# Causal mask of an attention kernel: maxima masked on VectorE by one add-and-max instruction, transposed scores masked by one fp32r matmul per head and step, batch loop unrolled

## What is computed

```
x = x + tanh(g_xattn) * wkv(w, u, layernorm(x), ctx)
s = layernorm(x);  h1 = rmsnorm(s, ln1);  h = rmsnorm(s, ln2)
scores = einsum('bqhd,bkhd->bhqk', h1 @ Wq.T, h1 @ Wk.T) / sqrt(32)     # 16 heads of 32
scores = where(causal, scores, finfo.min)
attn = (softmax(scores) @ v).reshape(b, s, d) @ Wo.T
mod = 0.1 * tanh(attn @ A)                                              # rank 16
gate = silu(h @ W_in.T + mod * (h @ A) @ B);  mlp = (gate * (h @ W_up.T)) @ W_down.T
x = x + tanh(g_ffn) * (s + mlp)
```

## Time and profile before

| | |
|---|---|
| device time, median of 3 runs | 1065.28 us (1063.98 to 1066.85) |
| span of the profiled execution, which is its own time here | 1067.0 us |
| TensorE busy | 946.0 us, 89% |
| VectorE busy | 641.0 us, 60% |
| ScalarE, GpSimd busy | 412.6 us and 343.2 us, 39% and 32% |
| mean granted clock | 0.933 |

### The profile page before, as it was taken

One profiled execution on the slowest core, in us unless ns is written; L12 is line 12 of the kernel. 1 busy time (PEld: TensorE's weight loads), 2 busy tenths in 40 slices (PEclk: granted clock), 3 DMA queues, 4 the chain that ended last, 5 costly groups with the idle time before them and its releaser, 6 DMA issues. The chain is left out here.

```text
span 1067.0 us, 13783 instructions
## 1 busy us (share of the span) xinstructions
PE 946.0 (89%) x4880; PEld 728.0 (68%) x4880; DVE 641.0 (60%) x1032; ACT 412.6 (39%) x725; POOL 343.2 (32%) x202
## 2 busy tenths in 40 slices
PE   3129999889899999898899999988899999999998
PEld 3127656777788766587688866677688875678886
DVE  7987653698456852678636864478835765232223
ACT  2406454222234555333233654333222555433331
POOL 7540011565440001365542001256544000254441
PEclk9559989899899989999899998999999998999999
DMA  9001213322222210522221220421222221122321
GB/s 280 32 1 40 47 35 112 107 63 85 90 89 72 61 41 2 188 79 70 89 81 49 81 66 18 150 97 60 89 78 78 72 52 41 50 89 94 102 80 42
DMA packets 33548, 81.37 MB, mean 76 GB/s; under 512 B 5648, under 2 KB 5648, under 8 KB 32400
## 3 DMA queue, kind: packets, MB, share of 16 engines
q1 hardware_dynamic: 33472, 80.41, 24.5%
HBM read 63.35 MB, written 4.19 MB: 63 GB/s over the span
## 5 line engine op out<-in xcount | busy, mean ns | idle before, releaser
L373 POOL TENSOR_TENSOR gu_lo<-raw_gu,gu_hi 128x1024 fp32r<-128x1024 f32 x64 | 153.2, 2394 | 589.4 <-ACT gu_hi L487 589.4
L913 PE MATMUL ps<-h_hi,gu_hi 128*128 128x512 f32 x512 | 205.6, 402 | 5.0 <-DVE gsil L867 5.0
L914 PE MATMUL ps<-h_lo,gu_hi 128*128 128x512 f32 x512 | 202.4, 395 | 0.0
L915 PE MATMUL ps<-h_hi,gu_lo 128*128 128x512 f32 x512 | 202.3, 395 | 0.0
L805 DVE TENSOR_REDUCE mx<-ps 128x1 f32<-128x512 f32 (+3 forms) x256 | 112.5, 484 | 74.3 <-PE ps L1006 73.6
L591 ACT ACTIVATE act_hi<-prod 128x512 fp32r<-128x512 f32 x64 | 40.4, 632 | 253.3 <-DVE prod L872 253.3
L867 DVE SCALAR_TENSOR_TENSOR gsil<-th,ps 128x512 f32<-128x512 f32 x64 | 43.3, 677 | 141.0 <-ACT th L587 141.0
L545 ACT ACTIVATE e_row<-ps 128x512 f32<-128x512 f32 (+1 forms) x192 | 90.8, 521 | 92.5 <-PE ps L1026 91.7
L377 POOL TENSOR_TENSOR wd_lo<-raw_d,wd_hi 128x512 fp32r<-128x512 f32 x64 | 94.1, 1470 | 90.4 <-ACT wd_hi L493 90.4
L913 PEld LDWEIGHTS ps<-h_hi,gu_hi 128*128 128x128 f32 x512 | 97.1, 190 | 30.2 <-DVE gsil L867 9.0
L915 PEld LDWEIGHTS ps<-h_hi,gu_lo 128*128 128x128 f32 x512 | 96.6, 189 | 22.7
(11 more groups left out here) (156 smaller groups left out, 1630.5 us busy)
## 6 DMA issues: line engine op xcount, KB each, us to landing
raw_gu<-w_gu_dram SPq DMA_DIRECT2D x64, 512.0 KB, 3.3
raw_d<-w_down_dram SPq DMA_DIRECT2D x64, 256.0 KB, 3.0
x_sb<-x_dram SPq DMA_DIRECT2D x16, 256.0 KB, 3.6
vT<-ctxT_dram SPq DMA_DIRECT2D x4, 1024.0 KB, 8.9
q_st<-q_st SPq DMA_DIRECT2D x16, 256.0 KB, 2.9
k_st<-k_st SPq DMA_DIRECT2D x16, 256.0 KB, 2.9
out_dram<-base SPq DMA_DIRECT2D x16, 256.0 KB, 2.1
q_st<-q_lo SPq DMA_DIRECT2D x32, 64.0 KB, 2.0
```

What stands on the lines that cost most here:

```text
L373: pool.tensor_tensor(gu_s[f % 2][1][:], raw_gu[f % 2][:], f32(gu_s[f % 2][0][:]), ALU.subtract).then_inc(gu_lo, 1)
L913: pe.matmul(dst, w_hi, m_hi, start=start, stop=False)
L914: pe.matmul(dst, w_hi, m_lo, start=False, stop=False)
L915: return pe.matmul(dst, w_lo, m_hi, start=False, stop=stop)
```

## The change

The mask matmuls of scores(n) go; VectorE adds the mask itself while it takes the maximum, with `tensor_tensor_reduce`: it reads the scores from PSUM and a bf16 mask row from SBUF, adds them, writes the sum back to PSUM, and puts the maximum into `mx`. The mask of scores_T becomes an fp32r matmul, one for both blocks of a step (256 columns) where there are two, and one for the one block (128 columns) where there is one: 48 a batch instead of 64. Only the first matmul of such a step clears its bank. The values of a head lie 17 columns apart instead of 32, which changes the layout of `v_aug`. All engines' loops over batches are unrolled.

```diff
-VW = 32
+VW = R + 1
+VROW = H * VW + 16
-MASKED = -1e30
+MASKED, LOWEST = -1e30, -3e38
+ST_FIRST = [0, P, 0]
...
-        identb = place("identb", [P, P], BF16)
-        mask_qk = place("mask_qk", [P, P], BF16)
-        mask_kq = place("mask_kq", [P, P], BF16)
+        ident_r = place("ident_r", [P, P], F32R)
+        mask_kq = place("mask_kq", [P, 2, P], F32R)
+        mask_row = place("mask_row", [P, T], BF16)
...
-        v_aug = place("v_aug", [P, TB, H, VW], F32)
+        v_aug = place("v_aug", [P, TB, VROW], F32)
...
 # on each of the five engines
-            with sp.Fori(0, NB - 1) as b:
-                batch(b, False)
-            batch(NB - 1, True)
+            for b in range(NB):
+                batch(b, b == NB - 1)
...
 # GpSimd, constants
-            pool.affine_select(out=mask_qk[:], in_=mask_qk[:], compare_op=ALU.is_ge, fill=MASKED, base=0,
+            pool.affine_select(out=mask_row[:, T - P:T], in_=mask_row[:, T - P:T], compare_op=ALU.is_ge, fill=MASKED, base=0,
...
+            pool.wait_ge(const_rdy, 3)
+            pool.tensor_copy(ident_r[:], ident[:]).then_inc(const_rdy, 1)
+            pool.memset(v_aug[:], 0.0).then_inc(pool_own, 1)
             pool.wait_ge(pool_own, 4)
-            pool.tensor_copy(identb[:], ident[:]).then_inc(const_rdy, 1)
-            pool.memset(v_aug[:], 0.0).then_inc(pool_own, 1)
-            pool.wait_ge(pool_own, 5)
-            pool.memset(v_aug[:, :, :, R:R + 1], 1.0).then_inc(const_rdy, 1)
+            for tb in range(TB):
+                op = pool.memset(v_aug[:, tb, 0:H * VW].rearrange("p (h r) -> p h r", r=VW)[:, :, R:VW], 1.0)
+            op.then_inc(const_rdy, 1)
...
 # ScalarE, values
-                    act.activation(v_aug[:, tb, :, 0:R], ps[:, bank, 0:H * R].rearrange("p (h r) -> p h r", r=R), ACT.Copy)
+                    act.activation(v_aug[:, tb, 0:H * VW].rearrange("p (h r) -> p h r", r=VW)[:, :, 0:R], ps[:, bank, 0:H * R].rearrange("p (h r) -> p h r", r=R), ACT.Copy)
...
 # VectorE, maxima
-                            op = dve.reduce_max(mx[:, qb, j:j + 1], ps[:, s_bank(n) + i, at:at + (qb + 1) * P], AX.X)
+                            w = (qb + 1) * P
+                            op = dve.tensor_tensor_reduce(ps[:, s_bank(n) + i, at:at + w], ps[:, s_bank(n) + i, at:at + w], mask_row[:, T - w:T], 1.0,
+                                                          LOWEST, ALU.add, ALU.max, mx[:, qb, j:j + 1])
...
 # TensorE, scores
-                            pe.matmul(ps[:, s_bank(n) + i, at:at + w], q_st[g % 3][0:96, j, blk(qb)], k_st[g % 3][0:96, j, 0:w], start=True, stop=False)
-                            op = pe.matmul(ps[:, s_bank(n) + i, at + w - P:at + w], identb[:], mask_qk[:], start=False, stop=True)
+                            op = pe.matmul(ps[:, s_bank(n) + i, at:at + w], q_st[g % 3][0:96, j, blk(qb)], k_st[g % 3][0:96, j, 0:w], start=True, stop=True)
...
 # TensorE, scores_T
-                                      q_st[g % 3][0:98, 2 * pr + i, kb * P:T], start=True, stop=False)
-                            op = pe.matmul(ps[:, st_bank(m) + i, at:at + P], identb[:], mask_kq[:], start=False, stop=True)
+                                      q_st[g % 3][0:98, 2 * pr + i, kb * P:T], start=at == ST_FIRST[s], stop=False)
+                        blocks = len(ST_STEPS[s])
+                        op = pe.matmul(ps[:, st_bank(m) + i, 0:blocks * P], ident_r[:], mask_kq[:, 0:blocks, :], start=False, stop=True)
                         op.then_inc(st_ps, 1)
...
 # TensorE, weigh
-                            op = pe.matmul(ps[quad(j), 6, kb * P:T], v_aug[:, kb, 4 * g + j, :], e_row[g % 2][:, j, E_AT[kb]:E_AT[kb] + w],
+                            op = pe.matmul(ps[quad(j), 6, kb * P:T], v_aug[:, kb, (4 * g + j) * VW:(4 * g + j) * VW + 32], e_row[g % 2][:, j, E_AT[kb]:E_AT[kb] + w],
```

More of the change, by code:

```diff
@@ L328, in _ @@
             pool.memset(ident[:], 0.0).then_inc(pool_own, 1)
-            pool.memset(mask_qk[:], 0.0).then_inc(pool_own, 1)
-            pool.memset(mask_kq[:], 0.0).then_inc(pool_own, 1)
+            pool.memset(mask_row[:], 0.0).then_inc(pool_own, 1)
+            pool.memset(f32(mask_kq[:]), 0.0).then_inc(pool_own, 1)
             pool.memset(minus_half[:], -0.5).then_inc(const_rdy, 1)
@@ L333, in _ @@
             pool.affine_select(out=ident[:], in_=ident[:], compare_op=ALU.not_equal, fill=1.0, base=0,
-                               pattern=[[-1, P]], channel_multiplier=1).then_inc(pool_own, 1)
-            pool.affine_select(out=mask_qk[:], in_=mask_qk[:], compare_op=ALU.is_ge, fill=MASKED, base=0,
                                pattern=[[-1, P]], channel_multiplier=1).then_inc(const_rdy, 1)
-            pool.affine_select(out=mask_kq[:], in_=mask_kq[:], compare_op=ALU.is_ge, fill=MASKED, base=0,
-                               pattern=[[1, P]], channel_multiplier=-1).then_inc(const_rdy, 1)
+            pool.affine_select(out=mask_row[:, T - P:T], in_=mask_row[:, T - P:T], compare_op=ALU.is_ge, fill=MASKED, base=0,
+                               pattern=[[-1, P]], channel_multiplier=1).then_inc(const_rdy, 1)
+            pool.affine_select(out=mask_kq[:], in_=f32(mask_kq[:]), compare_op=ALU.is_ge, fill=MASKED, base=0,
+                               pattern=[[0, 2], [1, P]], channel_multiplier=-1).then_inc(const_rdy, 1)
             pool.iota(steps[:], [[1, T]], base=0, channel_multiplier=0,
                       allow_small_or_imprecise_dtypes=True).then_inc(const_rdy, 1)
+            pool.wait_ge(const_rdy, 3)
+            pool.tensor_copy(ident_r[:], ident[:]).then_inc(const_rdy, 1)
+            pool.memset(v_aug[:], 0.0).then_inc(pool_own, 1)
             pool.wait_ge(pool_own, 4)
-            pool.tensor_copy(identb[:], ident[:]).then_inc(const_rdy, 1)
-            pool.memset(v_aug[:], 0.0).then_inc(pool_own, 1)
-            pool.wait_ge(pool_own, 5)
-            pool.memset(v_aug[:, :, :, R:R + 1], 1.0).then_inc(const_rdy, 1)
+            for tb in range(TB):
+                op = pool.memset(v_aug[:, tb, 0:H * VW].rearrange("p (h r) -> p h r", r=VW)[:, :, R:VW], 1.0)
+            op.then_inc(const_rdy, 1)
             pool.memset(tcols[:], 0.0).then_inc(const_rdy, 1)
@@ L426, in batch @@
                             scales_of_x1(b + 1)
-            with pool.Fori(0, NB - 1) as b:
-                batch(b, False)
-            batch(NB - 1, True)
+            for b in range(NB):
+                batch(b, b == NB - 1)
         @block.scalar
@@ L446, in _ @@
                 kexp_step(0, cb, True)
-            act.wait_ge(const_rdy, 9)
+            act.wait_ge(const_rdy, 10)
             act.wait_ge(woa_ps, 1)
@@ L599, in batch @@
                     normed(b + 1)
-            with act.Fori(0, NB - 1) as b:
-                batch(b, False)
-            batch(NB - 1, True)
+            for b in range(NB):
+                batch(b, b == NB - 1)
         @block.vector
@@ L728, in _ @@
             dve.tensor_scalar(half_gate[:], gate_t[:, 1:2], 0.5, None, ALU.mult)
-            dve.wait_ge(const_rdy, 5)
+            dve.wait_ge(const_rdy, 6)
             for cb in range(DB):
@@ L902, in batch @@
                 assert last or own["n"] == DVE_OWN_PER_BATCH, own["n"]
-            with dve.Fori(0, NB - 1) as b:
-                batch(b, False)
-            batch(NB - 1, True)
+            for b in range(NB):
+                batch(b, b == NB - 1)
         @block.tensor
@@ L940, in normed_T @@
                 op.then_inc(hnT_ps, 1)
-            pe.wait_ge(const_rdy, 6)
+            pe.wait_ge(const_rdy, 3)
             for cb in range(DB):
@@ L963, in _ @@
             pe.wait_ge(ones_rdy, 3)
-            pe.wait_ge(const_rdy, 8)
+            pe.wait_ge(const_rdy, 9)
             def batch(b, last):
@@ L1165, in batch @@
                 down(NF - 1)
-            with pe.Fori(0, NB - 1) as b:
-                batch(b, False)
-            batch(NB - 1, True)
+            for b in range(NB):
+                batch(b, b == NB - 1)
 def kernel(x, ctx_2048, g_xattn, g_ffn, L0_xattn_w, L0_xattn_u, L0_ffn_ln1_w, L0_ffn_ln2_w, L0_ffn_Wq, L0_ffn_Wk,
```

## The result

The changed kernel takes 1069.96 us (median of 9, 1069.12 to 1072.3), the kernel before 1065.28 (median of 9). The ratio is 1.0048, 95% interval 1.0031 to 1.0065: slower by half a per cent, where 1046 us was forecast. Runs more than 1.5% above the fastest of their kernel are left out of all ratios here, which concerns three runs of experiment 2 and no others.

What follows compares the result with a forecast made beforehand. TensorE was taken as the limit, VectorE co-limiting in steps 0 to 9. 5.4 us a batch gave 21.5, plus 0.9 loop, less 3.0 clock: 19.4 off 1067.0, less 1.7 to the median, 1046 us; range 1037 to 1054, chance 0.52.

Steps and rivals of the forecast that it cites:

- x = 0.10: VectorE: each add-and-max costs 0.10 us more than a plain reduction; 8.8 less 34 times that saves 5.4 a batch.
- x = 0: VectorE: delivering the reduced value adds nothing per instruction; 8.8 us saved a batch; with the clock held 1029 us, chance 0.13.
- Steps 10 to 15 are bound by TensorE ... together 2.9: Attention, steps 10 to 15: 2.04 us saved on scores and 0.84 on transposed scores, together 2.9 a batch.
- steps 18 to 20 run at the half clock ... doubled 2.5: Attention, steps 18 to 20: TensorE's saving of 1.26 us a batch counts double at the half clock, 2.5.
- Of its idle 2.56 us I keep 0.7, so 1.86 - 28x are saved: Steps 0 to 9: VectorE becomes the limit; 1.86 us a batch saved, less the added cost of 28 add-and-max instructions.
- so such a fall costs 1.5 ... 3 us lost: Scores phase: batch 1's clock fall costs 1.5 us and comes in batches 2 and 3 too, 3 us lost.
- Rival 2: Attention: clock falls more often as TensorE waits for VectorE, six more falls at 1.5 us, 1055 us; chance 0.14.
- Rival 3: Attention: VectorE becomes the bound, each add-and-max costing 0.28 us more through a drained read, 1072 us; chance 0.14.
- Rival 4: Attention: gains and losses cancel, TensorE's saving seen in busy time and nowhere in the span, 1062 to 1068; chance 0.07.
- The signs named beforehand: Prediction wrong if add-and-max adds above 0.24 us, an fp32r mask matmul exceeds 0.12, or clock falls where it now holds.
- The merged mask: Transposed scores: fp32r mask matmuls save 0.21 us a head over 64 heads, at 0.12 us per 256-column mask.
- The loop: Batch seams: unrolling brings gaps of 0.80 and 0.56 us to 0.24, saving 0.9 us in total.

Runs made afterwards that it cites:

- experiment 2: Changed kernel with reduce_max in place of the add-and-max and both masks' fill 0: 1058.4 us, median of six; ratio 0.9826 from three of them.
- before (12): Kernel before, unchanged, profiled a second time: one run of 1065.62 us, span 1063.8.
- experiment 5: Changed kernel plus 30 idle matmuls a batch where TensorE waited: 1049.07 us, ratio 0.9823 to the kernel before.
- experiment 7: Changed kernel with old score masks and reduce_max in steps 0 to 9, 16 and 17, plus 17 idle matmuls a batch: 1041.36 us, ratio 0.9759.
- experiment 9: Kernel before with loops unrolled, masks as they were, plus 17 idle matmuls a batch: 1051.53 us, ratio 0.9843.
- reduce_max, busy (10): Changed kernel with reduce_max, masks' fill 0 and 30 idle matmuls a batch: 1037.95 us, ratio 0.9725 to the kernel before.
- (3): Changed kernel with the transposed scores' masks as before, bf16 matmuls of 128 columns, one per block: 1075.23 us, ratio 1.0100 to the kernel before.
- (1): Kernel before with its five batch loops unrolled and nothing else: 1067.73 us, ratio 1.0037.

## Why the prediction was wrong

The starts of the batches, of scores, of transposed scores and of the first matmul of L1080 (other line numbers in the other kernels) cut each trace into stages. Their lengths, summed over the four batches (us, numbers of experiments in the heads; the columns add to the spans; the first row is the prologue and each batch's matmuls ahead of its first scores):

| stage | before | before (12) | changed | reduce_max (2) | busy (5) | hybrid, busy (7) | before, busy (9) | reduce_max, busy (10) |
|---|---|---|---|---|---|---|---|---|
| up to the first scores | 128.6 | 130.5 | 130.2 | 129.1 | 129.1 | 129.2 | 128.3 | 128.9 |
| steps 0 to 9 | 92.1 | 92.1 | 96.8 | 89.4 | 97.0 | 92.2 | 92.1 | 90.6 |
| steps 10 to 15 | 75.5 | 72.4 | 75.2 | 73.3 | 68.8 | 67.2 | 72.1 | 67.9 |
| steps 16 to 20 | 66.9 | 66.6 | 64.5 | 60.6 | 50.6 | 50.8 | 52.0 | 48.8 |
| steps 21 to 23 | 26.2 | 26.2 | 25.1 | 25.0 | 26.2 | 25.1 | 26.2 | 24.7 |
| tail | 85.8 | 85.8 | 84.0 | 85.3 | 89.1 | 84.0 | 85.8 | 84.1 |
| MLP stage | 591.9 | 590.1 | 594.1 | 591.1 | 588.6 | 590.9 | 594.2 | 591.7 |

With the clock held on both sides, the edit can be read against the terms of the sum (us over the four batches, minus is a gain; the forecast without its loop and clock terms):

| stage | forecast, x = 0.10 | as made (9 to 5) | forecast, x = 0 | reduce_max (9 to 10) | hybrid (9 to 7) |
|---|---|---|---|---|---|
| steps 0 to 9 | +3.8 | +4.9 | -7.4 | -1.5 | +0.1 |
| steps 10 to 15 | -11.6 | -3.3 | -11.6 | -4.2 | -4.9 |
| steps 16 to 20 | -8.4 | -1.4 | -10.0 | -3.2 | -1.2 |
| steps 21 to 23 | -3.2 | 0.0 | -4.0 | -1.5 | -1.1 |
| tail | -2.0 | +3.3 | -2.0 | -1.7 | -1.8 |
| sum | -21.4 | +3.5 | -35.0 | -12.1 | -8.9 |

Of the +3.5, 6.2 are the falls of experiment 5 in its last two stages (115.3 - 109.1), so the change as made gains some 3 us where 21 were forecast, or 16 without the doubling for the half clock in steps 18 to 20. The step of the prediction that failed is the sum of what TensorE saves: work taken from TensorE was counted as time nearly in full wherever TensorE looked like the limit. The lost clock, which the unrolled kernel before loses for the most part too, comes second.

Point by point:

- **The step that weighs most: "Steps 10 to 15 are bound by TensorE ... together 2.9" and "steps 18 to 20 run at the half clock ... doubled 2.5".** 11.6 and 10 us over four batches were forecast; in the changed kernel 0.3 and 2.4 came. With the clock held they are still only 3.3 and 1.4. Batch 2 of experiments 7 and 9 shows steps 10 to 15 matmul by matmul, 1.23 us less instead of 2.9. The masks of the scores were well priced: two heads of 256 columns take 0.24 us instead of 0.50. The masks of the transposed scores were not: 0.84 was forecast for these steps and 0.3 came, since the prices before had been taken from the scores (0.51 for a head with two blocks, 0.45 measured) and a merged mask costs 0.18, not 0.12. And TensorE, being quicker, now waits for VectorE's maxima where it had not waited, 0.8 us in all (experiment 7: the first three lines are TensorE's weight loads, the last is VectorE's):

```profile
616.53 0.30 PEld L1013 LDWEIGHTS ps<-k_st,q_st 96*128 96x128 f32 x2 [0.21 <-DVE mx L813]
617.18 0.30 PEld L1013 LDWEIGHTS ps<-k_st,q_st 96*128 96x128 f32 x2 [0.35 <-DVE mx L813]
...
622.53 0.19 PEld L1013 LDWEIGHTS ps<-k_st,q_st 96*128 96x128 f32 x1 [0.26 <-DVE mx L813]
...
615.13 0.69 DVE L790 TENSOR_TENSOR q_lo<-ps,qk_hi 128x512 fp32r<-128x512 f32 x1 [1.47 <-ACT qk_hi L519]
```

VectorE is idle for much of that window. But its program has one order, and ahead of the maxima of step 13 stands a subtraction (L790) that waits 1.47 us for ScalarE. An engine with a low busy share can still be the one that is waited for.
- **The same in steps 0 to 9: "Of its idle 2.56 us I keep 0.7, so 1.86 - 28x are saved".** Without the masks and at the old VectorE price (2) steps 0 to 9 take 22.34 a batch, 0.69 less than before, not 1.86: VectorE still idles 2.0 of them. In batch 2 of that trace 0.5 of it is at the start and 1.0 at step 6, where VectorE waits for the next group's scores, which TensorE issues behind the transposes of VectorE's own maxima. x was well sized, 0.057 to 0.067 where I took 0.10. The forecast of 28 x 0.10 - 1.86 = 0.94 us lost a batch stands against 1.17 in the table ((96.8 - 92.1) / 4): near, but by luck, as a saving 1.2 us too high met a price for x 0.9 us too high.
- **The clock: "so such a fall costs 1.5 ... 3 us lost".** In the changed kernel all four batches have 4 to 6 us at 1.2 GHz in steps 10 to 15, 10 to 14 us in steps 16 to 20 and 1 to 3 in steps 0 to 9, 75 us in the attention stages of its profile against 48 in that of the kernel before. Idle matmuls are worth 21 us to the changed kernel and 16 to the unrolled kernel before (1067.73 to 1051.53). So the change made the clock's loss larger by some 5 us by the medians, 3 by the ratios against the unrolled kernel and 7 against the looped one, where 3 were counted. Most of the 21 us was there to be won before the change.
- **The rivals.** Rival 2 named the mechanism at 0.14 and priced it at 9 us; it came, but smaller, and alone would have left the kernel faster. Rival 3 (VectorE the bound by a drained read, x = 0.28) has the right sign for the wrong reason: x was 0.06 to 0.07. Rival 4, gains and losses that cancel, with TensorE's saving "in its busy time and nowhere in the span", describes the result best: 13 us less busy, and 2 us above its range. It had 0.07.
- **The signs named beforehand.** An fp32r mask matmul of 256 columns costs 0.18, above 0.12, and falls came in steps 0 to 9, which held the clock before: two of the three signs that the prediction is wrong. The scores phase took 62.0 to 63.4 us instead of 56; with the clock held it takes 57.9 in the kernel before (9), 57.6 in the changed one (5) and 56.0 in the hybrid (7).
- **The merged mask** gave about 5 us where 13.4 were forecast (3).
- **The loop:** 0.24 us at each seam came as forecast. That unrolling the kernel before costs 0.4% (1) was not foreseen; its cause stays open.
- **The base of the sum:** the profile that it reads has two falls in steps 10 to 15 that the second profile of the kernel before hasn't. And the device time lies 1.8 us above the span (1065.62 and 1063.8 in 12), so a span of 1067.0 belongs to a time of about 1068.8 and not to its own length. The forecast of 1046 isn't touched by this, since the 1.7 us that it takes off bring it to the median of the runs again.
- Right: nothing came from GpSimd's constants or the layout of `v_aug` that the stages can tell, and the tail's 0.5 us a batch came (0.45).

## What to carry to other kernels

Before taking work from a TensorE that is nearly full, ask what it will wait for afterwards. Look at the other engine's queue and not at its busy share: VectorE, busy half of the time, was waited for because an instruction ahead of the maxima waited itself. The work removed turns into idle time there, and the idle time can cost the clock, which is paid in the next stage where TensorE is the bound again. Price a matmul by its own rows and neighbours; a price borrowed from a similar step was 0.06 us too high, 64 times over. Cut the profile by steps, put busy time and granted clock of each step side by side, and move work only in the steps whose receiving engine has room. If single runs of a kernel spread by 1% on one core, look for clock falls, and try idle matmuls in the known waits: here they gave the kernel before 1.6% with no other edit than unrolled loops. Do this before judging a change, on both kernels, so that the clock is out of the comparison.

## What the runs showed of the hardware

- The clock fell behind stretches in which TensorE still worked: 2.09 us busy and 14 matmuls in 3.3 us preceded 6.7 us at 0.50 (changed kernel, batch 2), while 2.62 us and 16 matmuls did not (kernel before).
- Idle matmuls into a bank that nobody reads, 30 a batch at 0.23 us, brought the changed kernel from 1070.0 to 1049.1 us; 17 a batch brought the unrolled kernel before from 1067.7 to 1051.5.
- A fall inside steps full of matmuls costs much: the same 129 matmuls took 18.0 us at 1.00 and 22.3 at 0.77.
- The add-and-max takes 707 ns for 512 elements and a plain reduction 688, though the first writes its sum back to PSUM; its accumulator read has a row of its own, 133 ns, of which 0.057 to 0.067 us is paid.
- A bf16 mask matmul of 128 columns between fp32r ones adds 0.04 us of its own, and the matmul behind it takes 0.08 us longer to the next start: 0.31 instead of 0.23 for 512 columns (experiment 9, batch 2, 611.42 to 611.77).
